# A two-layer graph kernel: one-hot stationary, gathered rows moving, node-major sums in groups of 8 tiles, a register load on TensorE with each tile

## The chip, the core and the metric

The kernel runs on one core of a Trainium2 chip. The core has five engines with a queue of instructions each: TensorE (PE; its weight loads are listed as PEld), VectorE (DVE), ScalarE (ACT), GpSimd (POOL) and SyncE (SP, which only issues transfers). They meet through semaphores. The metric is the device time of one execution in microseconds (us), the median of several runs.

## The reference, cut to what matters

There are 12500 nodes with 256 features and 200000 edges from `src` to `dst`, sorted by `dst`. Two layers follow each other; each ends in a residual and a layer norm:

```
# layer 0
t1  = x @ W1
msg = (t1[src] + (x[src] * x[dst]) @ W2) / (sqrt(deg[src]) * sqrt(deg[dst]))
agg = segment_sum(msg, dst)
x1  = layernorm(x + l2_normalise(leaky_relu(where(in_cnt > 0, t1 + agg, 0) + b0)))
# layer 1
out = segment_sum((x1 @ W.T + b1)[src], dst) / (in_deg + 1)
y   = layernorm(x1 + out)
```

Both layers reduce to one thing that is costly: for each edge a row of 256 float32 is fetched by `src`, and the rows of one `dst` are added. In layer 0 the fetched row is x divided by the root of its node's degree, in layer 1 it is x1. The matrix products come after the sum, once per node.

## The kernel before

**Tiles.** The edges are cut into tiles of 128, padded to 1568. A round is U = 32 tiles, and each layer has ROUNDS = 49 of them. One round belongs roughly to 256 nodes (two blocks of 128), since the edges are sorted.

**The gathers (POOL).** For each tile one indirect DMA (`gather_quarter`, L408) fetches 128 rows of 1 KB into one of the 32 places of `ring`. GpSimd reads the 128 row numbers from `idx`, a tile in SBUF. `idx` has 32 columns; ACT fills 8 of them at a time from `src_col` (`refill`, L523) as soon as TensorE has used the 8 tiles that stood in these places of the ring. The last round of a layer has FINAL = 27 tiles of gathers. The first 28 tiles of layer 0 are fetched unscaled from x, and with them their factors (`gather_r`, L416), before the scaled table is stored; the other 4 of round 0 come from the table.

**The sums (DVE, PE, DVE).** For a group of GT = 4 tiles DVE makes a one-hot tile of 64 columns each (`group_hot`, L715, both inputs in SBUF), TensorE multiplies (L1034): the gathered rows are the stationary operand, in two halves of 128 features, and the one-hot of 64 columns moves. The result is feature-major: 128 features by 64 nodes, for each half. DVE adds it to the accumulator `big` at a place that it loads into a register (`load_base`, L738; `add_group`, L743). Two buffers in PSUM take turns.

**The rest of layer 0.** In each round DVE also makes two batches of bf16 one-hots of dst's digits (`hot_batch`, L598, two instructions a batch), TensorE multiplies them (L940) and DVE adds the counts to `deg` (L829): this is the in-degree.

**The nodes.** One round later the sums of two blocks are finished: TensorE turns x (L997, L999), DVE mixes it with the sums (L753, L755), TensorE multiplies with the weights (`products`, L1013), DVE and ACT normalise (L768 to L823), SP stores. In layer 1, ACT copies the sums (L537) to be the stationary operand. Layer 1 starts when the last block of layer 0 is stored (POOL waits for SP, L327). TensorE multiplies all 32 tiles of the last round too; for the last 5 it only doesn't wait for a gather.

**What sets the order.** Each engine's program is written out by hand; nothing is planned by costs. Before the rounds (0 to 240 us) the edges are turned, degrees counted, x scaled and stored as a table.

Of the kernel before, what the change touches and what calls it, by code (L numbers as in the profile page):

```python
# [35 lines left out]
GT = 4  # L36
GR = U // GT
GROUPS = TILES // GT
WIN = 64
ACC_N = NPAD + WIN  # L40
# [8 lines left out]
HBATCHES = TILES // HB  # L49
# [6 lines left out]
LAST_K = 2  # L56
AHEAD = 3
HOTS = 4
QT = U // 4
# [4 lines left out]

RAW = 7 * GT
RAW_EARLY = [u for u in range(RAW) if 3 <= u < 13 or 20 <= u < 26]
RAW_LATE = [u for u in range(RAW) if u not in RAW_EARLY]
RAW_FIRST = 3
FIRST_GROUPS = 3
# [3 lines left out]
def gnn(nc, x, src, dst, w1, w2, b0, wl, b1, out):  # L73
# [3 lines left out]
    base_dram = nc.dram_tensor("group_bases", (BLOCKS * U,), I32, kind="Internal").ap()  # L77
    sums_dram = [nc.dram_tensor(f"sums{n}", (NPAD + P, D), F32, kind="Internal").ap() for n in range(2)]

    with ExitStack() as ctx:  # L80
# [3 lines left out]
        def sem(name):  # L84
# [3 lines left out]
        big = sb("big", [P, KF * ACC_N])  # L88
        acc = big[:, :].rearrange("p (k n) -> p k n", k=KF)
        x_all = big[:, 0:NW * D].rearrange("p (w f) -> p w f", w=NW)  # L90
        ring = sb("ring", [P, U, D])
# [7 lines left out]
        src_digits = ring_flat[:, 2 * BLOCKS * P:3 * BLOCKS * P].bitcast(BF16)  # L99
        lo = [src_digits[:, 0:TILES], sb("dst_lo", [P, TILES + HB], BF16)[:, :]]  # L100
        hi = [src_digits[:, TILES:2 * TILES], sb("dst_hi", [P, TILES + HB], BF16)[:, :]]
        count_to = sb("count_to", [P, P, PAIR], BF16)
        hot = sb("hot", [P, 2, HB // PAIR, P + HI, PAIR], BF16)
# [3 lines left out]
        steps = ring_flat[:, 4 * BLOCKS * P:].bitcast(BF16)[:, 0:3 * SB * (P + HI)].rearrange(  # L107
            "p (n t j) -> p n t j", n=3, t=SB)
        step_digits = nat[0][:, 0:2 * STEP_TILES].rearrange("p (d t) -> p d t", d=2)
        digit_t = hot[:, :, :, :, :].rearrange("p a b c d -> p (a b c d)")[:, 0:2 * TILES].bitcast(I32)  # L110
        win_iota = sb("win_iota", [P, WIN])
        dst_hot = sb("dst_hot", [P, HOTS, GT, WIN])
# [5 lines left out]
        zeros = sb("zeros", [P, D])  # L118
        dump_row = sb("dump_row", [P, 1])
        epsilon = sb("epsilon", [P, 1])  # L120
        bounds = sb("bounds", [P, 2, BLOCKS])
        gmin = sb("gmin", [BLOCKS, U])
        gmax = sb("gmax", [BLOCKS, U])
        floor_i = sb("floor_i", [BLOCKS, U], I32)
        floor_late = sb("floor_late", [BLOCKS, U // GR, GR - LAST_K - 1], I32)
        floor_f = sb("floor_f", [BLOCKS, U])
        gmin_i = sb("gmin_i", [BLOCKS, U], I32)
        bad = sb("bad", [BLOCKS, 4])
        flag = sb("flag", [1, 1], I32)
        base_row = sb("base_row", [1, BLOCKS * U], I32)  # L130
        base_row_f = dst_hot[0:1, 0:2, :, :].rearrange("p a b c -> p (a b c)")[:, 0:BLOCKS * U]
# [3 lines left out]
        r_diag = [sb(f"r_diag{n}", [P, P]) for n in range(2)]  # L135
        columns = r_diag[0]
        deg = sb("deg", [P, NW])
# [6 lines left out]
        a_t = [sb(f"a_t{n}", [P, KF, P]) for n in range(2)]  # L144
        out_t = [sb(f"out_t{n}", [P, D]) for n in range(2)]
        sums_t = sb("sums_t", [P, D])
        sum_a = a_t
        xa = [sb(f"xa{n}", [P, KF, P]) for n in range(2)]
# [11 lines left out]
        def group_sum(buf):  # L160
            return banks[:, 2 * buf:2 * buf + 2, 0:WIN]
# [3 lines left out]
        turned = [banks[:, 5 + s, :].rearrange("p (a k n) -> p a k n", a=2, k=KF) for s in range(2)]  # L165
        project = [banks[:, 7, 0:D], banks[:, 5, 0:D]]
# [38 lines left out]
        raw_turn = sem("raw_turn")  # L205

        r_edges_in = [sem(f"r_edges_in{n}") for n in range(2)]
# [18 lines left out]
        x_turned = sem("x_turned")  # L226
        sums_turned = sem("sums_turned")
        mixed = sem("mixed")
        hist_added = sem("hist_added")
# [878 lines left out]
```

## Time and profile before

| what | value |
|---|---|
| timed runs | median 4266.98 us of 3 (4265.9 to 4276.45) |
| profiled execution | 4292.12 us, span of its instructions 4290.4 us |
| busy PE | 3621.7 us (84%), PEld 3168.4 (74%) |
| busy POOL | 3140.3 us (73%) |
| busy DVE | 1600.2 us (37%) |
| busy ACT | 381.6 us (9%) |
| DMA | 489.92 MB, 114 GB/s over the span |
| mean granted TensorE clock | 0.595 of 2.4 GHz |

The profiled execution is slower than the median of the timed runs by 25.1 us; its durations are used against its own time. "Busy" counts an engine's instructions without their issue; a busy share is an average over stages. For POOL the span between two gathers is not counted as busy. The chain of waits says which work ended last, step by step, and that is what an edit has to shorten. The first 240 us are preparation, layer 0's rounds run from there to about 2271 us, layer 1's to the end.

### The profile page before, as it was taken

The numbers are of one execution on the slowest core, as the hardware profiler recorded it, in microseconds if no ns is written. First come the engines' busy times: TensorE is split into PE (matmuls) and PEld (weight loads), VectorE is DVE, ScalarE is ACT, GpSimd is POOL, SyncE is SP. The second block draws the span as 40 slices with busy tenths as digits, with TensorE's granted clock in tenths as the row PEclk, the third lists the DMA queues.
The fourth block names the chain that finished last, engine by engine and source line by source line (L and its number), as shares of the span: only waits on it lengthen the run. The fifth ranks groups of instructions, "written<-read, shape, count | busy, mean of one in ns | idle before, by whom it ended". The sixth has DMA issues, their size and how long they took to land.

```text
span 4290.4 us, 60042 instructions
## 1 busy us (share of the span) xinstructions
PE 3621.7 (84%) x17483; PEld 3168.4 (74%) x17483; DVE 1600.2 (37%) x4104; ACT 381.6 (9%) x1359; POOL 3140.3 (73%) x3175
## 2 busy tenths in 40 slices
PE   6578888888888888888887888888888888888888
PEld 5477777877777777777776777777777777767776
DVE  9954444444444444444442222222222222222222
ACT  8800000000000000000000000000000000000000
POOL 2277777777777777777776777777777777777776
PEclk8755656666566656666565555555555555555555
DMA  5243333333333333343433344343343433434433
GB/s 164 87 129 115 111 115 113 112 115 110 115 110 116 111 114 115 110 115 109 116 109 98 112 117 117 112 116 113 116 117 112 117 114 114 118 111 117 117 113 104
DMA packets 236973, 489.92 MB, mean 114 GB/s; under 512 B 57537, under 2 KB 136916, under 8 KB 236948
## 3 DMA queue, kind: packets, MB, share of 16 engines
q0 software_dynamic: 150944, 409.95, 33.6%
q1 hardware_dynamic: 86004, 79.66, 5.8%
q8 instruction: 13, 0.21, 0.0%
q14 instruction: 12, 0.10, 0.0%
HBM read 450.84 MB, written 38.54 MB: 114 GB/s over the span
## 4 chain that ended last, share of the span: by engine, by line
POOL 69%; issue 25%; DVE 3%; PE 2%; POOLq 1%; DMA 0%; DVEq 0%; SPq 0%; ACT 0%; ACTq 0%
POOL ring L408 68%; DVE hot L598 2%; PE banks L1034 1%; POOL r_edge L416 1%; POOLq L444 0%; POOL ring L412 0%; PE banks L940 0%; POOLq L405 0%; PE banks L1013 0%; POOLq L406 0%; DVEq L590 0%; DVEq L640 0%; DMA ring<-in_dst 0%; PE banks L999 0%; DMA ring<-scaled_x,idx 0%
## 5 line engine op out<-in xcount | busy, mean ns | idle before, releaser
L1034 PE MATMUL banks<-dst_hot,ring 128*128 128x64 f32 x12544 | 2949.5, 395 | 562.5 <-DMA ring<-x,idx 250.8
L1034 PEld LDWEIGHTS banks<-dst_hot,ring 128*128 128x128 f32 x12544 | 2576.2, 294 | 938.3 <-DMA ring<-x,idx 377.0
L408 POOL DMA_INDIRECT ring<-x,idx x1563 | 1525.4, 976 | 499.2 <-issue 476.2
L408 POOL DMA_INDIRECT ring<-scaled_x,idx x1535 | 1539.4, 1003 | 467.9 <-issue 467.3
L743 DVE TENSOR_TENSOR big<-banks,big 128x128 f32 x784 | 228.7, 292 | 1936.8 <-PE banks L1034 1934.7
L715 DVE TENSOR_TENSOR dst_hot<-win_iota,dst_rel 128x256 f32<-128x256 f32 x787 | 337.0, 428 | 311.1 <-issue 310.9
L523 ACT COPY idx<-src_col 128x8 int32 (+1 forms) x392 | 77.5, 198 | 2875.4 <-PE banks L1034 2875.3
L940 PE MATMUL banks<-hot 128*128 128x98 bf16 x2848 | 210.7, 241 | 47.9 <-DVE hot L598 47.1
L940 PEld LDWEIGHTS banks<-hot 128*128 128x128 bf16 x2848 | 194.1, 120 | 67.6 <-DVE hot L598 44.8
L1013 PE MATMUL banks<-wt_s,a_t 128*128 128x256 f32 x392 | 179.0, 637 | 1.3 <-ACT a_t L537 1.3
L598 DVE TENSOR_TENSOR hot<-ring,count_to 128x2048 bf16<-128x2048 bf16 (+1 forms) x160 | 162.0, 1094 | 0.2
L491 ACT ACTIVATE ring<-r_diag,ring 128x128 bf16<-128x128 f32 x576 | 161.3, 389 | 4.6 <-DVE ring L634 4.6
L412 POOL DMA_INDIRECT ring<-in_x,idx x28 | 38.7, 1381 | 155.0 <-DVE r L663 133.1
L598 DVE TENSOR_TENSOR hot<-dst_lo,count_to 128x2048 bf16<-128x2048 bf16 x99 | 121.9, 1231 | 72.4 <-issue 72.3
L1013 PEld LDWEIGHTS banks<-wt_s,a_t 128*128 128x128 f32 x392 | 125.6, 335 | 27.8 <-ACT a_t L537 1.5
L1013 PE MATMUL banks<-w_s,xa 128*128 128x256 f32 x392 | 121.2, 438 | 0.0
L1013 PE MATMUL banks<-w_s,a_t 128*128 128x256 f32 x392 | 106.8, 397 | 0.0
L999 PE MATMUL banks<-r_diag,x_t 128*128 128x128 f32 x392 | 102.8, 417 | 0.0
L598 DVE TENSOR_TENSOR hot<-dst_hi,count_to 128x1568 bf16<-128x1568 bf16 x99 | 95.9, 969 | 0.0
L999 PEld LDWEIGHTS banks<-r_diag,x_t 128*128 128x128 f32 x392 | 95.4, 333 | 0.0
L1013 PEld LDWEIGHTS banks<-w_s,a_t 128*128 128x128 f32 x392 | 82.1, 209 | 14.0
L1013 PEld LDWEIGHTS banks<-w_s,xa 128*128 128x128 f32 x392 | 80.9, 218 | 10.1
(118 smaller groups left out, 1043.4 us busy)
## 6 DMA issues: line engine op xcount, KB each, us to landing
ring<-x,idx POOLq DMA_INDIRECT x1563, 2.8
ring<-scaled_x,idx POOLq DMA_INDIRECT x1535, 2.8
x<-out_t SPq DMA_DIRECT2D x98, 128.0 KB
x_t<-x SPq DMA_DIRECT2D x98, 128.0 KB, 2.2
big<-in_x SPq DMA_DIRECT2D x1, 12416.0 KB
x_t<-in_x SPq DMA_DIRECT2D x97, 128.0 KB, 2.2
result<-out_t SPq DMA_DIRECT2D x97, 128.0 KB
scaled_x<-big SPq DMA_DIRECT2D x6, 1792.0 KB, 13.8
```

The source lines that it names most:

```text
L408: g.indirect_dma_start(ring[:, u, :], None, table[layer], bass.IndirectOffsetOnAxis(ap=idx[:, u:u + 1], axis=0)).then_inc(rows_in[u], 16)
L412: g.indirect_dma_start(ring[:, u, :], None, x, bass.IndirectOffsetOnAxis(ap=idx[:, u:u + 1], axis=0)).then_inc(rows_in[u], 16)
L416: g.indirect_dma_start(r_edge[:, u:u + 1], None, r_dram, bass.IndirectOffsetOnAxis(ap=idx[:, u:u + 1], axis=0)).then_inc(r_edges_in[n], 16)
L491: last = nc.scalar.activation(steps[:, third, t, first:first + size], columns[:, 0:size], ACT.Sign, bias=step_digits[:, digit, bass.ds(n * ...
L523: nc.scalar.copy(idx[:, q * QT:(q + 1) * QT], src_col[:, bass.ds(i * U + U + q * QT, QT)]).then_inc(idx_ready, 1)
L598: last = nc.vector.tensor_tensor(hots[half], vals.unsqueeze(2).to_broadcast(shape), count_to[:, 0:size, :].unsqueeze(1).to_broadcast(shape ...
L715: last = nc.vector.tensor_tensor(dst_hot[:, buf, :, :], win_iota[:, :].unsqueeze(1).to_broadcast([P, GT, WIN]), rel, ALU.is_equal)
L743: nc.vector.tensor_tensor(here, group_sum(k % 2), here, ALU.add).then_inc(groups_added, 1)
L940: last = nc.tensor.matmul(hist, lo_hot[half][:, t // PAIR, :, t % PAIR], hi_hot[half][:, t // PAIR, :, t % PAIR], start=first and t == 0, ...
L999: last = nc.tensor.matmul(turned[s][:, 1, k, :], x_t[s][:, k * P:(k + 1) * P], r_diag[s][:, :], start=True, stop=True)
L1013: last = nc.tensor.matmul(project[s], left, right, start=k == 0, stop=k == len(parts) - 1)
L1034: last = nc.tensor.matmul(group_sum(k % 2)[:, f, :], ring[:, u, f * P:(f + 1) * P], dst_hot[:, k % HOTS, j, :], start=j == 0, stop=j == GT ...
```

## The change

- The one-hot becomes the stationary operand (128 edges by 128 nodes), and the gathered row moves (257 columns: 256 features and a column of ones, set once in `ring`, whose places are now 264 wide). One float32 matmul a tile instead of two. The sums come out node-major, and column 256 counts the edges of a node, so the batches of bf16 one-hots, their matmuls and `deg` go in the rounds.
- A group is GT = 8 tiles, 4 groups a round. `group_hot` makes 8 one-hots of 128 columns in one instruction of 1024 elements; its first input is now a row in PSUM (`lane_row`), and what is compared is dst's low 7 bits. A group of 8 may span two blocks of 128 nodes: `add_group` adds it to both, with a mask for each, in two instructions of 257 elements. Four PSUM buffers take turns.
- x is no longer turned and mixed feature-major. DVE mixes in node-major form (`mix`), TensorE turns the mixed halves (`turn_halves`, after tile 20 of a round), ACT copies them from PSUM (`take_turned`), and TensorE multiplies (`products`, after tile 24).
- Round 0 of layer 0 is fetched unscaled as a whole (32 tiles, and 32 gathers of factors behind `r_stored`).
- The last round's matmuls stop with its 27th tile.
- After each tile, TensorE loads one register from memory (`pace`); the value isn't used.

```diff
-GT = 4
+GT = 8
-WIN = 64
+DW = D + 1
+PITCH = 264
-LAST_K = 2
+LAST_K = 1
+TURN_U = 20
+MIX_U = 24
+SUMS = 4
-RAW = 7 * GT
+RAW = U
...
         def group_sum(buf):
-            return banks[:, 2 * buf:2 * buf + 2, 0:WIN]
+            return banks[:, buf, 0:DW]
...
             g.wait_ge(step_digits_made, 1)
-            for u in RAW_EARLY:
-                gather_raw(u)
-            g.wait_ge(r_made, 1)
-            for u in RAW_LATE[:RAW_FIRST]:
+            for u in range(RAW):
                 gather_raw(u)
             g.wait_ge(r_stored, 16)
-            for u in RAW_LATE[:RAW_FIRST] + RAW_EARLY:
-                gather_r(u, 0)
-            for u in RAW_LATE[RAW_FIRST:]:
-                gather_raw(u)
-            for u in RAW_LATE[RAW_FIRST:]:
-                gather_r(u, 1)
+            for u in range(RAW):
+                gather_r(u)
...
             def refill(layer, i, q):
 
-                act.wait_ge(tiles_done, (layer * ROUNDS + i) * U + q * QT + QT + U)
+                act.wait_ge(groups_done, group_no(layer, i, q) + 1)
...
+            def take_turned(layer, m):
+                parts = 2 if layer == 0 else 1
+                for s in range(2):
+                    act.wait_ge(halves_turned, 2 * node_no(layer, m) + s + 1)
+                    if s == 0:
+                        act.wait_ge(projected, 2 * node_no(layer, m) + 2)
+                    act.sem_inc(act_turn, 1)
+                    nc.scalar.copy(a_t[s][:, 0:parts, :, :].rearrange("p h k n -> p (h k n)"),
+                                   turned[s][:, 0:parts * D]).then_inc(a_ready[s], 1)
...
             def group_hot(first_tile, buf, raw=False):
 
-                rel = dst_rel[:, bass.ds(first_tile, GT)].unsqueeze(2).to_broadcast([P, GT, WIN])
+                rel = dst_rel[:, bass.ds(first_tile, GT)].unsqueeze(2).to_broadcast([P, GT, P])
                 last = nc.vector.tensor_tensor(dst_hot[:, buf, :, :],
-                                               win_iota[:, :].unsqueeze(1).to_broadcast([P, GT, WIN]),
+                                               lane_row.unsqueeze(1).to_broadcast([P, GT, P]),
                                                rel, ALU.is_equal)
...
-            def add_group(layer, i, k, base):
-                v.wait_ge(tiles_done, group_no(layer, i, k) * GT + GT + U)
-                here = acc[:, :, bass.ds(base, WIN)]
-                nc.vector.tensor_tensor(here, group_sum(k % 2), here, ALU.add).then_inc(groups_added, 1)
+            def add_group(layer, i, k, block):
+
+                v.wait_ge(groups_done, group_no(layer, i, k) + 1)
+                for n in range(2):
+                    here = big[:, bass.ds((block + n) * DW, DW)]
+                    last = nc.vector.scalar_tensor_tensor(here, group_sum(k), here_mask[:, n, bass.ds(i * GR + k, 1)],
+                                                          here, ALU.mult, ALU.add)
+                last.then_inc(groups_added, 1)
+
+            def mix(m, sums):
+
+                two = bass.ds(2 * m, 2)
+                nc.vector.scalar_tensor_tensor(pair[0], sums[:, :, D], 0.0, r[:, two], ALU.is_gt, ALU.mult)
                 for s in range(2):
+                    v.wait_ge(x_in[s], 16 * (m + 1))
+                    nc.vector.scalar_tensor_tensor(halves[:, s, 0, :], x_t[s][:, :], root[:, bass.ds(2 * m + s, 1)],
+                                                   sums[:, s, 0:D], ALU.mult, ALU.add)
+                    nc.vector.tensor_tensor(halves[:, s, 1, :], x_t[s][:, :], sums[:, s, 0:D],
+                                            ALU.mult).then_inc(mixed, 1)
...
                     ordered()
-
-                    if layer == 0 and k in (0, 3):
-                        half = k // 3
-                        hot_batch(SRC_BATCHES + 2 * i + half + 1, 2 * i + half + 1, 1 - half, 1)
-                    if layer == 0 and k % 4 == 1:
-                        add_hist(SRC_BATCHES + 2 * i + k // 4)
...
+                    if finish and k >= LAST_K:
+                        done = acc[:, bass.ds(2 * i - 2, 2), :]
+                        if k == LAST_K and layer == 0:
+                            mix(i - 1, done)
+                        if k == LAST_K + 1:
+                            finish_sums(layer, i - 1, done)
+                            moments(layer, i - 1)
+                        if k == LAST_K + 2:
+                            norm(layer, i - 1)
...
+            def pace():
+
+                pe.value_load(block_row[0:1, 0:1], min_val=0, max_val=NW - 1)
...
                 for k in range(GR):
-                    if layer == 0 and k in (0, GR // 2):
-                        half = k // (GR // 2)
-                        dst_hist(SRC_BATCHES + 2 * i + half, half)
                     pe.wait_ge(dst_hot_made, group_no(layer, i, k) + 1)
                     pe.wait_ge(groups_added, group_no(layer, i, k) + 1)
-                    for j in range(GT):
-                        u = k * GT + j
-                        if u < end:
-                            rounds_before = layer * (ROUNDS if u < FINAL else ROUNDS - 1) + i
-                            pe.wait_ge(rows_in[u], 16 * (rounds_before + 1))
-                        for f in range(KF):
-                            last = nc.tensor.matmul(group_sum(k % 2)[:, f, :], ring[:, u, f * P:(f + 1) * P],
-                                                    dst_hot[:, k % HOTS, j, :], start=j == 0, stop=j == GT - 1)
-                        last.then_inc(tiles_done, 1)
...
+                    tiles = range(k * GT, min((k + 1) * GT, end))
+                    for u in tiles:
+                        rounds_before = layer * (ROUNDS if u < FINAL else ROUNDS - 1) + i
+                        pe.wait_ge(rows_in[u], 16 * (rounds_before + 1))
+                        last = nc.tensor.matmul(group_sum(k), dst_hot[:, k % HOTS, u - k * GT, :], ring[:, u, 0:DW],
+                                                start=u == tiles[0], stop=u == tiles[-1])
+                        if u == tiles[-1]:
+                            last.then_inc(groups_done, 1)
+                        pace()
+                        if finish and u == TURN_U - 1:
+                            turn_halves(layer, i - 1)
+                        if finish and u == MIX_U - 1:
+                            products(layer, i - 1)
```

How the instructions stand on VectorE in the loop over layer 0's rounds, from the top of a round, first before (one group of 4 tiles with a batch of bf16 one-hots; ISA and REGISTER_ALU rows are waits, signals and register work; `hot` is that batch, `base_row` the register load):

```order
L715 TENSOR_TENSOR dst_hot<-win_iota,dst_rel 128x256
L741 REGISTER_ALU
L743 ISA
L743 TENSOR_TENSOR big<-banks,big 128x2x64
L738 ISA
L738 TENSOR_LOAD base_row
L738 ISA x2
L594 ISA
L598 ISA
L598 TENSOR_TENSOR hot<-dst_lo,count_to 128x8x256
L598 REGISTER_ALU
L598 TENSOR_TENSOR hot<-dst_hi,count_to 128x8x196
```

and now, one group of 8 tiles (`hot_space` holds the one-hots, `banks` is PSUM):

```order
L710 TENSOR_TENSOR hot_space<-banks,dst_rel 128x1024
L733 REGISTER_ALU
L736 ISA
L736 SCALAR_TENSOR_TENSOR big<-banks,here_mask,big 128x257
L736 ISA
L736 REGISTER_ALU
L736 SCALAR_TENSOR_TENSOR big<-banks,here_mask,big 128x257
L729 ISA
L729 TENSOR_LOAD block_row
L729 ISA x2
```

The batch is gone, the one-hot instruction is longer and its first input is in PSUM, and the add is two instructions. On TensorE in the same loop, before, two groups with what stands between them (turning x):

```order
L1034 MATMUL banks<-dst_hot,ring 128x64 x8
L994 ISA
L995 REGISTER_ALU
L997 MATMUL banks<-ident,x_t 128x128 x2
L999 MATMUL banks<-r_diag,x_t 128x128 x2
L997 MATMUL banks<-ident,x_t 128x128 x2
L999 MATMUL banks<-r_diag,x_t 128x128 x2
```

and now, around the turn in the middle of the third group (the waits are on the rows in the ring and on the mixed halves):

```order
L1004 MATMUL banks<-ring,hot_space 128x257
L993 TENSOR_LOAD block_row
L993 ISA x2
L971 ISA
L977 MATMUL banks<-ident,halves 128x128 x4
L971 REGISTER_ALU
L977 MATMUL banks<-ident,halves 128x128 x4
```

Each tile is one matmul row instead of two, and each is followed by a register load and two more instructions of the sequencer.

## Rows read from the trace of the kernel before

**Rows 1.** The page, chain that ended last, shares of the span.

```profile
POOL 69%; issue 25%; DVE 3%; PE 2%; POOLq 1%; DMA 0%; DVEq 0%; SPq 0%; ACT 0%; ACTq 0%
```

**Rows 2.** Waits of POOL: us in total, times, longest.

```profile
POOL ring L408 <- issue: 943.6, 3095, 0.3
POOL ring L412 <- DVE r L663: 133.1, 1, 133.1
POOL ring L408 <- SPq L327: 22.9, 1, 22.9
```

**Rows 3.** Line L408, all gathers of the rounds: duration min/median/max, first and last start.

```profile
L408 POOL DMA_INDIRECT ring<-x,idx x1563: 945/949/1217, 2270.6 to 4271.3; - x196
L408 POOL DMA_INDIRECT ring<-scaled_x,idx x1535: 945/949/1972, 240.7 to 2246.8; - x192
```

**Rows 4.** The page, costliest groups: busy us, mean ns, idle before.

```profile
L408 POOL DMA_INDIRECT ring<-x,idx x1563 | 1525.4, 976 | 499.2 <-issue 476.2
L408 POOL DMA_INDIRECT ring<-scaled_x,idx x1535 | 1539.4, 1003 | 467.9 <-issue 467.3
```

**Rows 5.** Timeline of layer 0, 302 to 307 us, POOL and DVE: start, us.

```profile
302.83 0.43 DVE L715 TENSOR_TENSOR dst_hot<-win_iota,dst_rel 128x256 f32<-128x256 f32 x1 [1.42 <-issue]
302.97 1.11 POOL L408 DMA_INDIRECT ring<-scaled_x,idx  x1 [0.30 <-issue]
...
304.09 1.23 DVE L598 TENSOR_TENSOR hot<-dst_lo,count_to 128x2048 bf16<-128x2048 bf16 x1 [0.62 <-issue]
304.39 1.75 POOL L408 DMA_INDIRECT ring<-scaled_x,idx  x1 [0.31 <-issue]
...
306.44 0.94 POOL L408 DMA_INDIRECT ring<-scaled_x,idx  x1 [0.30 <-issue]
306.49 0.29 DVE L743 TENSOR_TENSOR big<-banks,big 128x128 f32 x1
```

**Rows 6.** Timeline of layer 0, 655 to 658 us, POOL and DVE.

```profile
656.45 0.88 DVE L768 SCALAR_TENSOR_TENSOR e<-banks,scal,b_s 128x256 f32<-128x256 f32 x2
656.48 0.95 POOL L408 DMA_INDIRECT ring<-scaled_x,idx  x1 [0.30 <-issue]
```

**Rows 7.** Timeline, a round of layer 0: the slow gathers of 1028 to 1040 us.

```profile
1031.80 1.14 POOL L408 DMA_INDIRECT ring<-scaled_x,idx  x1 [0.30 <-issue]
...
1037.01 1.01 POOL L408 DMA_INDIRECT ring<-scaled_x,idx  x1 [0.30 <-issue]
```

**Rows 8.** The page, DVE's one-hots of the groups.

```profile
L715 DVE TENSOR_TENSOR dst_hot<-win_iota,dst_rel 128x256 f32<-128x256 f32 x787 | 337.0, 428 | 311.1 <-issue 310.9
```

**Rows 9.** Timelines of PE: four tiles of layer 0; products of layer 1.

```profile
1004.03 3.64 PE L1034 MATMUL banks<-dst_hot,ring 128*128 128x64 f32 x16
...
2989.85 3.73 PE L1013 MATMUL banks<-wt_s,a_t 128*128 128x256 f32 x8
```

**Rows 10.** Register loads by line: duration ns min/median/max, first and last start.

```profile
L738 DVEq FUSED_REGOPS  x1456: 57/190/194, 235.1 to 4276.9; - x182
L738 DVEq TENSOR_LOAD <-base_row x784: 299/305/329, 234.7 to 4276.6; - x196
...
L1047 PEldq TENSOR_LOAD <-flag x1: 1094/1094/1094, 209.3 to 209.3; - x1
```

**Rows 11.** Timeline, start of the rounds.

```profile
231.44 0.36 DVE L715 TENSOR_TENSOR dst_hot<-win_iota,dst_rel 128x256 f32<-128x256 f32 x1
...
232.36 7.09 PE L1034 MATMUL banks<-dst_hot,ring 128*128 128x64 f32 x32 [12.19 <-DVE dst_hot L723]
...
246.71 0.95 POOL L408 DMA_INDIRECT ring<-scaled_x,idx  x1 [0.30 <-issue]
```

**Rows 12.** Timeline, from layer 0 to layer 1.

```profile
2249.99 5.38 PE L1034 MATMUL banks<-dst_hot,ring 128*128 128x64 f32 x24 [0.57 <-DMA ring<-scaled_x,idx]
...
2261.43 0.48 DVE L768 SCALAR_TENSOR_TENSOR e<-banks,scal,b_s 128x256 f32<-128x256 f32 x1 [1.24 <-PE banks L1013]
...
2270.63 0.95 POOL L408 DMA_INDIRECT ring<-x,idx  x1 [22.93 <-SPq L327]
```

More of the change, by code:

```diff
@@ L48 @@
 PAIR = 2
-HBATCHES = TILES // HB
 SB = 4
@@ L441, in _ @@
                         g.wait_ge(table1_whole, 1)
[L442 to L443 removed]
+                    if layer == 1:
+                        for q in range(4):
+                            gather_quarter(layer, 0, q)
                     with g.Fori(1, ROUNDS - 1) as i:
@@ L872, in _ @@
                     if layer == 0:
-                        for s in range(2):
-                            mix(ROUNDS - 1, s, acc[:, :, (NW - 2 + s) * P:(NW - 1 + s) * P])
-                    for step in (finish_sums, moments, norm):
-                        step(layer, ROUNDS - 1)
+                        mix(ROUNDS - 1, acc[:, NW - 2:NW, :])
+                    finish_sums(layer, ROUNDS - 1, acc[:, NW - 2:NW, :])
+                    moments(layer, ROUNDS - 1)
+                    norm(layer, ROUNDS - 1)
             with v.Else():
@@ L1003, in products @@
-            def products(layer, m, s, taken):
-                if layer == 0:
-                    pe.wait_ge(mixed, 2 * m + 2 if s == 1 else 2 * m + 1)
-                    parts = [(xa[s][:, k, :], w2_s[:, k, :]) for k in range(KF)]
-                    parts += [(sum_a[s][:, k, :], w1_s[:, k, :]) for k in range(KF)]
-                else:
-                    pe.wait_ge(a_ready[s], taken + 1)
-                    parts = [(a_t[s][:, k, :], wt_s[:, k, :]) for k in range(KF)]
-                for k, (left, right) in enumerate(parts):
-                    last = nc.tensor.matmul(project[s], left, right, start=k == 0, stop=k == len(parts) - 1)
-                last.then_inc(projected, 1)
@@ L1016, in dst_hist, with turn_halves @@
-            def dst_hist(n, half):
-                pe.wait_ge(hist_added, n - SRC_BATCHES + 1)
-                hist_batch(n, half, True, True)
+            def turn_halves(layer, m):
+                for s in range(2):
+                    if layer == 0:
+                        pe.wait_ge(mixed, 2 * m + s + 1)
+                    elif s == 0:
+                        pe.wait_ge(sums_taken, m + 1)
+                    for h in range(2 if layer == 0 else 1):
+                        for k in range(KF):
+                            place = (h * KF + k) * P
+                            last = nc.tensor.transpose(turned[s][:, place:place + P], halves[:, s, h, k * P:(k + 1) * P],
+                                                       ident[:, :])
+                    last.then_inc(halves_turned, 1)
@@ new lines, in products @@
+            def products(layer, m):
+                weights = (w1_s, w2_s) if layer == 0 else (wt_s,)
+                for s in range(2):
+                    pe.wait_ge(a_ready[s], node_no(layer, m) + 1)
+                    parts = [(a_t[s][:, h, k, :], w[:, k, :]) for h, w in enumerate(weights) for k in range(KF)]
+                    for n, (left, right) in enumerate(parts):
+                        last = nc.tensor.matmul(project[s], left, right, start=n == 0, stop=n == len(parts) - 1)
+                    last.then_inc(projected, 1)
@@ L1037, in round_ @@
-                    if finish and layer == 0 and k == LAST_K:
-                        for s in range(2):
-                            turn_x(i - 1, s)
-                    if finish and k == LAST_K + 1:
-                        for s in range(2):
-                            products(layer, i - 1, s, i - 1)
+                    tiles = range(k * GT, min((k + 1) * GT, end))
[11 more added lines that the diff above has]
+                            products(layer, i - 1)
```

359 lines of the change are left out of this document (148 added, 211 removed).

## Prediction

> **What bounds the kernel now.** I read the chain of waits first [rows 1]: POOL holds 69% of it and its issue another 25%. The list of POOL's waits [rows 2] says that it is never fed late in the rounds: behind the preparation (133.1 us, once) the only long wait is 22.9 us between the layers; the other 943.6 us are 3095 gaps of about 0.305 us between one gather and the next. So the time is a row of gathers, and the view by line [rows 3] gives the clean step: median 949 ns plus 305 ns, 1.254 us. 1535 gathers lie between 240.7 and 2246.8 us, 1563 between 2270.6 and 4271.3.
>
> The means [rows 4] are above the median: 1003 ns in layer 0 and 976 in layer 1. That is (1003 − 949) × 1535 = 82.9 us and (976 − 949) × 1563 = 42.2 us of stretched gathers. The clean step plus this stretch gives back both stretches of time: 1534 × 1.254 + 82.9 = 2006.6 us against 2246.8 − 240.7 = 2006.1, and 1562 × 1.254 + 42.2 = 2000.9 against 2000.7. Nothing else is in them.
>
> What stretches a gather is seen in the timeline [rows 5]. The gather that starts at 302.97, while DVE's L715 (both inputs in SBUF) runs to 303.26, takes 1.11 us; the one at 304.39, with L598 running to 305.32, takes 1.75. The excess over 0.949 fits a wait until about where the DVE instruction ends. The gather at 306.44 beside L743, whose first input is in PSUM, takes 0.94, and the one at 656.48 beside the long L768 (0.88 us, input in PSUM) takes 0.95 [rows 6]. So a DVE instruction holds a gather up only when it reads two tensors in SBUF, as far as these rows go.
>
> TensorE is busy 84% of the time but not bounding: four tiles of 16 passes take 3.64 us [rows 9], 0.91 a tile, below 1.254.
>
> **The change part by part.**
>
> *Number of gathers and first start.* Layer 0's round 0 is now all unscaled. Its gathers of rows fall in POOL's 133.1 us of waiting [rows 2]; the 32 gathers of factors end, by my estimate of 1.25 us each, just ahead of the tables' being ready. Round 1's first gather needs group 0's matmuls. Before, the matmuls of 8 tiles started at 232.36, took 7.09, and round 1's fetching starts at 246.71, behind 4 gathers for round 0 [rows 11]. Now: memsets done as before at about 231.44, a one-hot of 1024 elements, 4 times that of 256. L715's 256 elements take 428 ns in the mean, 337.0 / 787 [rows 8], 0.36 here; 4 times 0.36 less fixed cost is 1.26 us, and two of them give 234.0. Then 8 tiles of matmuls: before each tile took 4 passes of 64 columns, now 2 of 257, and products of 256 columns take 3.73 / 8 = 0.47 us a pass with their end [rows 9], so about the same 7.1 for 16 passes. With ACT's refill and the issue that is 242. Gain 4.7 us.
>
> *Layer 0's row of gathers.* From round 1 there are 47 × 32 + 27 = 1531 gathers, 1530 steps × 1.254 = 1918.6 us. The batches L598 and the one-hots L715 with two SBUF inputs are gone; the new one-hot and both adds have one tensor in PSUM. What still reads two in SBUF is some 10 small instructions a round (in `mix` and the norm). Their price I take from a round of layer 0 where two gathers away from L598 and L715 took 1.14 and 1.01 us [rows 7]: 0.19 + 0.06 = 0.25 us over the 6 such instructions of a round, 0.04 each. 10 × 49 × 0.04 = 20 us. Bounds: 0, and 42.2 us over layer 1's 490 two-input instructions of before, 0.086 each, so 42 us. I take 20, since the small ones are the nearest kin.
>
> *Layer 1's.* 1562 × 1.254 = 1958.7; 2 such instructions a round, 98 × 0.04 = 4 us, bounds 0 and 8.4.
>
> *The register load on TensorE.* The trace before has no such load with each tile. DVE's L738 does the same (a value of a row in SBUF) 784 times at 299 to 329 ns with a 190 ns instruction behind it; TensorE's own, L1047, is there once, 1094 ns, at 209.3 us in the traffic of the preparation [rows 10]. A tile then costs TensorE's queue 0.31 + 0.19 us and the issue of a matmul and a wait, 0.15 to 0.4 by estimate: 0.65 to 0.9, beside two passes of 257 columns, at most 2 × 0.47 = 0.93 by L1013 [rows 9], and I take 0.86, since the 3.73 us hold the end of the last pass too. If load and passes lay behind one another it would be 0.31 + 0.86 = 1.17 and more; if beside, 0.9. Nothing in the load needs the array, so I take 0.9. A round of layer 0 holds 32t plus 8.5 us for the turn (8 transposes, 1.7 by estimate) and the products (16 passes, 6.8 at 0.43); POOL needs 32 × 1.254 + 0.4 = 40.5. At t = 0.9 that is 37.3: cover of 3 us. The cover ends at t = 1.0 in layer 0; in layer 1 (4.6 us of extra) at 1.11. Stalls within a round are buffered by the ring: 24 tiles × 1.254 = 30 us of rows ahead, less 2.8 for landing.
>
> The Trainium skill, page "DMA: Bandwidth & Descriptors", section "Latency and other measured facts", gives a register load from memory a floor of about 600 ns. The trace disagrees: 784 loads at 299 to 329 ns on VectorE [rows 10], and the measurement decides. With 0.6 + 0.19 + 0.35 one would have t = 1.14 and, by the sum of the first rival below, about 4,430 us.
>
> *DVE and ACT off the path.* The adds and one-hots are hidden: in a round of 40 us DVE has 4 × (1.26 + 2 × 0.4) us (0.29 for L743's 128 elements [rows 5], so about 0.4 for 257) and some 10 us for the nodes. ACT is called per 8 tiles as before.
>
> *Between the layers.* Before: the last tiles' matmuls start at 2249.99 for 5.38 (24 passes, with 5 empty tiles that go now), the norm at 2261.43, the first gather of layer 1 at 2270.63 [rows 12]: 20.6 from 2249.99. Now the last pair's path has its sums first on DVE and then turned: products and finish of the pair before 2.5 + 5.5, one-hot 1.3, adds 0.9, factors 1.2, mix 1.2, transposes 1.0, ACT's copy 0.6, products 5.2 (16 passes, at most 7.5 by L1013's 3.73 for 8 and half of that at the higher clock), and 9.2 from the norm (2270.63 − 2261.43): 28.6. So +8 us (+5 to +12): 23.8 becomes about 32.
>
> *End.* 4290.4 − 4271.3 = 19.1 us, unchanged by the same counting (−1 to +7).
>
> *Sum.* 242 + 1918.6 + 20 = 2180.6; + 32 = 2212.6; + 1958.7 + 4 = 4175.3; + 19.1 = 4194.4, 96 us under the span of 4290.4. With 1.7 us around the span the profiled time is 4196.1. The medians stand to that as 4266.98 / 4292.12 = 0.9941: 4171.5 us, I say 4171. With no stretch, 4147; with the upper prices and the gap and tail at their worst, 4202. Own range 4140 to 4202.
>
> **The rivals.**
>
> 1. *TensorE becomes the bound through the register load* (slower side). Place: between two tiles in its queue. It decides above t = 1.0, in layer 0 alone at first, and from t = 1.06 the kernel is no longer faster: 49 × (32 × 1.06 + 8.5 − 40.5) = 95 us, the whole gain. Above 1.11 each 0.1 us of t costs 64 × 49 × 0.1 = 314 us. With load and passes in series, t = 1.17: 4171 + 49 × (64 × 1.17 + 8.5 + 4.6 − 40.5 − 40.2) = 4,528. With L1047's 1.094 behind some 0.5 us, t = 1.6: 4171 + 49 × 34.8 = 5,876. For it: the only load on this engine was 1.09 us, and nothing shows that a load and passes run side by side. Against: 784 loads at 0.3, and that one lay in heavy traffic. Chance 0.12. A mild form, t from 1.0 to 1.06, ends at 4175 to 4265: 0.08.
> 2. *The new long one-hot holds POOL up after all.* Its `dst_rel` is in SBUF and it runs 1.26 us, 392 times; if the PSUM operand doesn't free the path, each hit costs half its length by the rows of L598 [rows 5], 0.31 to 0.63 us: 123 to 250 us, 4,290 to 4,417. For: L743's case is a short instruction. Against: L768's at 0.88 us [rows 6]. Chance 0.07.
> 3. *The stretch isn't DVE's but there anyway* (traffic): then only start and gaps change, and the time is 4171 + 101 = about 4,272, no change. Against: the excess ends with the DVE instruction. It is in the remaining 0.03.
>
> **How the numbers follow.** The forecast has 0.70, so 4171. Within 0.3%, about 13 us either way, a measurement of this kernel can't tell from no change; faster means under 4254. The forecast's 0.70, three quarters of the mild form and a little of the rest give 0.77; same 0.04; slower 0.12 + 0.07 = 0.19. The range of 8 in 10 is 4135 to 4260: the forecast's own and the mild form, 0.78, and the edges.
>
> **What would show it.** Right: L408's median at 0.95 and means below 0.97 in both layers, POOL's only waits the one before round 1 and one of about 32 us between the layers, round 1's first gather near 242, and TensorE's loads near 0.3 us with its steps of tiles following POOL's 1.25. Wrong: POOL waiting for ACT's `idx` behind TensorE's groups throughout, which is rival 1; gathers of over 1.3 us beside the one-hot of 1024 elements, rival 2; a mean of 1003 still there with neither, rival 3. Steps of tiles of TensorE with load and passes in series at over 1.0 us would make it wrong even with short loads.

## The result: 2.2% faster, and the profile after

The kernel after the change takes 4174.5 us (median of 4 runs, 4171.9 to 4178.56), the kernel before beside it 4269.35 (4265.9 to 4276.45). The ratio is 0.9777, 95% interval 0.976 to 0.9794. The forecast was 4171, faster. The profiled execution took 4172.7 us, its span 4170.9.

The page of the kernel after, its chain of waits by engine, answers to [rows 1]:

```profile
POOL 68%; issue 25%; DVE 4%; PE 1%; DVEq 1%; POOLq 1%; DMA 0%; SPq 0%; ACT 0%; ACTq 0%
```

It is the same row of gathers. The next lines are the waits of POOL after (total us, times, longest), which answer to [rows 2]:

```profile
POOL ring L405 <- issue: 941.5, 3091, 0.3
POOL r_edge L413 <- DMA r_table<-e: 102.7, 1, 102.7
POOL ring L405 <- SPq L327: 29.8, 1, 29.8
POOL ring L409 <- DVE halves L629: 14.3, 1, 14.3
POOL ring L405 <- ACT idx L514: 10.7, 2, 10.4
```

After the start, POOL waits only between the layers. Then the gathers themselves by line (min/median/max, first and last start), against [rows 3]:

```profile
L405 POOL DMA_INDIRECT ring<-x,idx x1563: 942/946/1211, 2190.5 to 4151.9; - x196
L405 POOL DMA_INDIRECT ring<-scaled_x,idx x1531: 942/946/1227, 238.8 to 2159.7; - x192
```

and their sums and means from the page, against [rows 4], with the new one-hot:

```profile
L405 POOL DMA_INDIRECT ring<-x,idx x1563 | 1486.5, 951 | 505.7 <-issue 475.9
L405 POOL DMA_INDIRECT ring<-scaled_x,idx x1531 | 1455.9, 951 | 476.4 <-issue 465.6
...
L710 DVE TENSOR_TENSOR hot_space<-banks,dst_rel 128x1024 f32<-128x1024 f32 x395 | 483.7, 1224 | 198.1 <-issue 197.6
```

The means fell from 1003 and 976 ns to 951: of 82.9 + 42.2 us of stretch, (951 − 946) × 3094 = 15.5 us are left. The longest gather is 1.23 us where it had been 1.97.

The forecast's sum, term by term (us; "after" from the first and last starts above and the span):

| part | forecast | after |
|---|---|---|
| first gather of round 1 | 242 | 238.8 |
| layer 0's row, first to last start | 1938.6 | 1920.9 |
| last gather of layer 0 to first of layer 1 | 32 | 30.8 |
| layer 1's row | 1962.7 | 1961.4 |
| last gather to the end | 19.1 | 19.0 |
| span | 4194.4 | 4170.9 |

The span was forecast 23.5 us too long. The forecast then took 24.6 us off again by the factor 0.9941, since the profiled execution of before was that much slower than its median. The profiled execution of after is not slower (4172.7 against 4174.5). So the nearness of 4171 to 4174.5 is two misses that cancel: the mechanism was right, and each of the two sizes was about 24 us, 0.6%, off. That nearness is luck.

### The profile page after: what moved, and what is told of

It reads as the page before. It is cut to its first block, busy times and chain, and to the rows that moved or that the text cites. A ratio compares the mean times of both kernels' runs of the same rounds, so it can differ in the third digit from the quotient of the medians.

```text
span 4170.9 us, 49033 instructions
## 1 busy us (share of the span) xinstructions
PE 3387.3 (81%) x9623; PEld 1749.8 (42%) x9623; DVE 1603.1 (38%) x3315; ACT 460.4 (11%) x1457; POOL 3033.6 (73%) x3179
## 4 chain that ended last, share of the span: by engine, by line
POOL 68%; issue 25%; DVE 4%; PE 1%; DVEq 1%; POOLq 1%; DMA 0%; SPq 0%; ACT 0%; ACTq 0%
POOL ring L405 68%; DVE hot_space L600 2%; DVEq L592 0%; PE banks L1004 0%; DVE big L663 0%; PE banks L988 0%; POOLq L435 0%; POOLq L402 0%; PE banks L916 0%; DVE big L724 0%; POOLq L403 0%; DVEq L635 0%; DMA ring<-in_dst 0%; SPq L270 0%; DMA ring<-x,idx 0%
## 5 line engine op out<-in xcount | busy, mean ns | idle before, releaser
L1004 PE MATMUL banks<-ring,hot_space 128*128 128x257 f32 x6252 | 2901.9, 575 | 671.6 <-DMA ring<-x,idx 326.5
L1004 PEld LDWEIGHTS banks<-ring,hot_space 128*128 128x128 f32 x6252 | 1315.7, 256 | 2192.9 <-DMA ring<-x,idx 1045.3
L405 POOL DMA_INDIRECT ring<-x,idx x1563 | 1486.5, 951 | 505.7 <-issue 475.9
L736 DVE SCALAR_TENSOR_TENSOR big<-banks,here_mask,big 128x257 f32 x784 | 343.7, 480 | 2086.7 <-PE banks L1004 2086.6
L710 DVE TENSOR_TENSOR hot_space<-banks,dst_rel 128x1024 f32<-128x1024 f32 x395 | 483.7, 1224 | 198.1 <-issue 197.6
L482 ACT ACTIVATE dst_rel<-columns,halves 128x128 bf16<-128x128 f32 x576 | 161.3, 374 | 4.5 <-DVE halves L629 4.5
L977 PE MATMUL banks<-ident,halves 128*128 128x128 f32 x588 | 131.2, 388 | 13.2 <-DVE halves L748 8.7
L977 PEld LDWEIGHTS banks<-ident,halves 128*128 128x128 f32 x588 | 112.8, 207 | 46.6 <-issue 23.0
L916 PE MATMUL banks<-hot_space 128*128 128x98 bf16 x1280 | 91.1, 236 | 40.0 <-DVE hot_space L600 39.2
L536 ACT COPY a_t<-banks 128x512 f32<-128x512 f32 (+1 forms) x196 | 90.4, 479 | 282.6 <-PE banks L977 282.2
L600 DVE TENSOR_TENSOR hot_space<-src_lo,count_to 128x2048 bf16<-128x2048 bf16 x80 | 97.6, 1221 | 0.2
L760 DVE SCALAR_TENSOR_TENSOR e<-banks,scal,b_s 128x256 f32<-128x256 f32 x98 | 42.9, 479 | 134.2 <-PE banks L988 134.2
```

The costliest lines, as they stand in the source:

```text
L405: g.indirect_dma_start(ring[:, u, 0:D], None, table[layer], bass.IndirectOffsetOnAxis(ap=idx[:, u:u + 1], axis=0)).then_inc(rows_in[u], 16)
L482: last = nc.scalar.activation(steps[:, third, t, first:first + size], columns[:, 0:size], ACT.Sign, bias=step_digits[:, digit, bass.ds(n * ...
L536: nc.scalar.copy(a_t[s][:, 0:parts, :, :].rearrange("p h k n -> p (h k n)"), turned[s][:, 0:parts * D]).then_inc(a_ready[s], 1)
L600: last = nc.vector.tensor_tensor(hots[half], vals.unsqueeze(2).to_broadcast(shape), count_to[:, 0:size, :].unsqueeze(1).to_broadcast(shape ...
L710: last = nc.vector.tensor_tensor(dst_hot[:, buf, :, :], lane_row.unsqueeze(1).to_broadcast([P, GT, P]), rel, ALU.is_equal)
L736: last = nc.vector.scalar_tensor_tensor(here, group_sum(k), here_mask[:, n, bass.ds(i * GR + k, 1)], here, ALU.mult, ALU.add)
```

## The experiments

Twelve kernels were run, in three lots on three chips, each lot with the kernel before beside it: 4269.0 us in the first, 4272.0 in the second, 5097.7 in the third. Ratios are to that one, with 95% intervals.

**1. Where the inputs of VectorE's instructions lie.** The kernel after, with the one operand moved back to SBUF:

```diff
-        lane_row = banks[:, 7, 0:P]
+        lane_row = sb("lane_sb", [P, P])[:, :]
```

> The kernel after with the first input of the one-hot (L710) in SBUF in place of PSUM, so that it reads two tensors in SBUF; nothing else. My theory: a gather that begins beside it waits until it ends; 392 of 1.22 us, a gather begins every 1.25, so nearly each is hit once and waits some 0.6 us: + 230 us, about 4,400, half in each layer, with gathers of 1.0 to 2.1 us beside L710. Rival (what stretched gathers before was the length, the bf16 type or chance traffic and not where the inputs lie): 4174.

Measured: 4285.6 us, ratio 1.0047 (1.0031 to 1.0062), that is + 111 us against the 4174.5 of the first result, and all of the change's gain is gone. The page of this kernel, its gathers and the one-hot; below it two pieces of its timeline (start, duration in us):

```profile
L405 POOL DMA_INDIRECT ring<-x,idx x1563 | 1520.2, 973 | 504.8 <-issue 475.8
L405 POOL DMA_INDIRECT ring<-scaled_x,idx x1531 | 1536.0, 1003 | 472.0 <-issue 465.6
...
L710 DVE TENSOR_TENSOR hot_space<-lane_sb,dst_rel 128x1024 f32<-128x1024 f32 x395 | 484.0, 1225 | 197.6 <-issue 197.1
```

```profile
1018.51 1.23 DVE L710 TENSOR_TENSOR hot_space<-lane_sb,dst_rel 128x1024 f32<-128x1024 f32 x1 [0.19 <-issue]
1018.71 1.85 POOL L405 DMA_INDIRECT ring<-scaled_x,idx  x1 [0.31 <-issue]
...
1039.29 1.22 DVE L710 TENSOR_TENSOR hot_space<-lane_sb,dst_rel 128x1024 f32<-128x1024 f32 x1 [1.23 <-issue]
1039.84 1.50 POOL L405 DMA_INDIRECT ring<-scaled_x,idx  x1 [0.30 <-issue]
```

The one-hot takes as long as with the operand in PSUM (1225 and 1224 ns), but the gather that starts 0.20 us behind it takes 1.85 us, the one 0.55 behind it 1.50: both end 0.82 and 0.83 us after the one-hot does (1019.74 and 1040.51). The direction is the theory's, the price half of what it said, and it isn't split evenly between the layers. I had spread the hits evenly over the instruction (0.6 us each), while the one-hot starts at a few places against the gathers. Counted in the trace, 194 gathers began beside it in layer 0, with 0.54 us of it left in the mean, and took 0.41 us more than the median of 0.946; in layer 1 it was 194 too, with 0.28 us left, and they took 0.17 more. That is 79 + 33 = 113 us, the whole of what the operand cost.

Then the same from the other side, on the kernel before: its batches left out (TensorE and the add go on with old one-hots, so these kernels leave out layer 0's in-degrees, which the outputs need), its one-hot with a first input in PSUM, and both.

```diff
-                        hot_batch(SRC_BATCHES + 2 * i + half + 1, 2 * i + half + 1, 1 - half, 1)
+                        v.wait_ge(hot_used, SRC_BATCHES + 2 * i + half + 2)
+                        v.sem_inc(hot_made, 1)
```

> The kernel before without the two bf16 one-hot instructions of each batch in the rounds (98 x 2 of layer 0; TensorE's matmuls and the add of counts stay and work on old one-hots, so the in-degrees are not computed). My theory: the gathers that waited for them get 61.6 us back in layer 0 and nothing in layer 1: about 4208. Rival (gathers are long because of traffic): 4269.

```diff
-        project = [banks[:, 7, 0:D], banks[:, 5, 0:D]]
+        project = [banks[:, 6, 0:D], banks[:, 5, 0:D]]
+        win_row = banks[:, 7, 0:WIN]
...
-                                               win_iota[:, :].unsqueeze(1).to_broadcast([P, GT, WIN]),
+                                               win_row.unsqueeze(1).to_broadcast([P, GT, WIN]),
...
+            nc.vector.tensor_copy(win_row, win_iota[:, :])
...
-                    pe.wait_ge(mixed, 2 * m + 2 if s == 1 else 2 * m + 1)
+                    pe.wait_ge(mixed, 2 * m + 2)
```

> The kernel before with the first input of its one-hot (L715 of before) in PSUM; the product of the first block goes to another bank for it and waits for both mixed blocks. My theory: the waits beside L715 go, 9 us in layer 0 and 39 in layer 1: about 4221. Rival: 4269.

> Both edits of the kernel before at once (in-degrees not computed). My theory: the two gains add, 62 + 48 = 110 us: about 4160, that is slightly below the kernel after, with the old number of matmuls, no register loads and the old gap between the layers. If the gain of the change lay in its matmuls or node-major sums, it would stay at 4210 or above.

Measured: without the batches 4217.6 us, 0.9869 (0.9854 to 0.9884), − 54; with the operand in PSUM 4216.3, 0.9864 (0.9849 to 0.9879), − 56; both 4169.5, 0.9757 (0.9743 to 0.977), − 102.5. The pages' gather rows, first without the batches, then with the operand in PSUM, then both:

```profile
L408 POOL DMA_INDIRECT ring<-x,idx x1563 | 1523.6, 975 | 500.3 <-issue 475.7
L408 POOL DMA_INDIRECT ring<-scaled_x,idx x1535 | 1472.8, 959 | 467.8 <-issue 466.9
```

```profile
L409 POOL DMA_INDIRECT ring<-scaled_x,idx x1535 | 1510.3, 984 | 467.7 <-issue 467.4
L409 POOL DMA_INDIRECT ring<-x,idx x1563 | 1482.8, 949 | 502.2 <-issue 476.0
```

```profile
L409 POOL DMA_INDIRECT ring<-x,idx x1563 | 1482.1, 948 | 501.5 <-issue 475.9
L409 POOL DMA_INDIRECT ring<-scaled_x,idx x1535 | 1460.8, 952 | 467.6 <-issue 467.3
```

Without the batches only layer 0's mean falls (1003 to 959); with the operand in PSUM layer 1's falls most (976 to 949), though layer 0's falls too (1003 to 984), more than the 9 us that I had given it. The single gains, 54 and 56 us, were expected as 62 and 48, and together they gave a little less than their sum of 110. Counted gather by gather in the trace of the kernel before, those that began beside a batch (L598) in layer 0 lost 65 us, those beside the one-hot (L715) 9 us in layer 0 and 40 in layer 1: 115 of the 125 us of stretch. Both together bring the kernel before, with its old matmuls, its old sums and no register loads, to 4169.5 us: within the intervals as fast as the kernel after. This shows where the 2.2% came from: no batches, and the one-hot's row in PSUM. The new shape of the product gave time only in that it needs no batches; the row in PSUM could be had without it.

**2. The register load on TensorE.** None, two and three in place of one behind each tile; with two:

```diff
                         pace()
+                        pace()
```

> The kernel after without the register load behind each tile. My theory: POOL alone sets the time, so 4174 us, within 5 us either way, and means of L405 of 951 ns as before. Rival: the load gives something back (it keeps TensorE's clock up, 0.72 against 0.60 before, or spaces its reads of SBUF away from the gathers); then without it the granted clock falls to about 0.60 and either the gaps between the layers and at the end grow by some 2 to 5 us each (4180), or gathers get longer again (4200 and more).

> Two register loads behind each tile. A load with its two followers takes 302 + 146 + 18 = 466 ns of TensorE's queue, a tile step in a burst is 0.66 us in the kernel after, so 1.13 here. My theory (loads and passes side by side, the ring as buffer): layer 0's round takes 32 x 1.13 + 6.5 = 42.7 us against POOL's 40.1, layer 1's about 40.2, so + 2.6 x 49 = 127 us: about 4300, POOL waiting for idx in layer 0 and hardly in layer 1. Rival 1: TensorE has slack up to 1.25 a tile because turn and products overlap the loads: 4174. Rival 2: loads and passes behind one another, 0.86 + 0.93: about 5,600.

> Three register loads behind each tile: t = 0.66 + 2 x 0.466 = 1.59. My theory: (32 x 1.59 + 6.5 - 40.1) + (32 x 1.59 + 4 - 40.1) = 32.1 us over both layers' rounds, x 49 = 1573: about 5,750, every further 0.466 us costing 64 x 49 x 0.466 = 1461 us. Rival (serial): about 7,000.

Measured: none 4168.6 us, 0.9768 (0.9754 to 0.9781); two 4556.9, 1.0678 (1.0662 to 1.0695); three 6594.2, 1.5453 (1.5425 to 1.5481). None and one are not told apart: the intervals of the ratios overlap, though the slowest of five executions without the load (4170.7) is below the fastest of four with it (4171.9), in another lot. The unchanged kernel was run once more to settle these 6 us (part 3) and met a slow chip, so they stay open. The profiled spans are 4169.0 and 4170.9 us, the mean granted clocks 0.713 and 0.719. So the load doesn't raise the clock either; that it is above the 0.595 of before comes with the other edits.

Two and three cost far more than I had said (4300 and 5750). The waits of POOL with two, and with three:

```profile
POOL ring L405 <- issue: 887.2, 2803, 4.6
POOL ring L405 <- ACT idx L514: 404.3, 290, 14.1
```

```profile
POOL ring L405 <- ACT idx L514: 2422.2, 377, 18.7
...
POOL ring L405 <- issue: 867.6, 2716, 9.1
```

and the loads with two, in 5 us of layer 0's rounds (ns min/median/max, first and last start in us):

```profile
L993 PEldq TENSOR_LOAD <-block_row x8: 298/301/302, 994.3 to 999.0; - x8
L993 PEldq FUSED_REGOPS  x8: 146/146/146, 994.6 to 999.4; - x8
L993 PEldq SEQ_ASSERT  x7: 18/18/18, 994.8 to 998.9; - x7
```

Eight loads start from 994.3 to 999.0, 0.67 us apart, though the three instructions of one last only 0.465 us together: the spaces between them belong to the price. With two loads a tile takes 2 × 0.67 = 1.34 us, and the gathers' starts say the same: layer 0's 1530 steps take 2092.8 us, 1.37 each, layer 1's 1562 take 2113.7, 1.35; with three it is 2.02 and 1.99. My step had been 1.13, from durations alone. A round of 32 such tiles would be 42.9 us, and 32 steps measured 43.8 and 43.3: the turn and the products, which I had added with 6.5 us, lie nearly all beside the queue's time. That these steps are the queue's and not the passes' is seen at the start of the rounds, where the rows lie ready. Without a load 80 passes, 40 tiles, take 20.21 us there, 0.51 us a tile, while with one load a tile takes 0.68:

```profile
231.42 20.21 PE L1004 MATMUL banks<-ring,hot_space 128*128 128x257 f32 x80 [20.68 <-DVE hot_space L717]
```

So TensorE has two limits a tile, about 0.5 us for its passes and 0.67 us of its queue for each load, and it binds when the larger passes POOL's 1.25. With one load nothing is near that.

**3. One idle VectorE instruction more,** behind each of the 392 one-hots, to compare kinds of instruction; the operands lie in a part of SBUF that the rounds don't use. One of these lines is added (`s_a` and `s_b` are `src_lo` and `src_hi` read as float32):

```diff
+                    nc.vector.tensor_tensor(s_a, s_a, s_b, ALU.mult)
...
+                    nc.vector.tensor_scalar(s_a, s_b, 1.0, None, ALU.mult)
...
+                    nc.vector.tensor_tensor(src_lo[:, :], src_lo[:, :], src_hi[:, :], ALU.mult)
```

> The kernel after once more, unchanged, beside the three below on one chip: ratio to the kernel before 0.977 to 0.979, 4170 to 4178 us. If it comes nearer 0.9768, the 6 us between the first result and the kernel without the register load were noise.

> The kernel after with one idle VectorE instruction more behind each of the 392 one-hots: a float32 product of two SBUF tensors of 784 elements, 0.9 us; its result is not used. My theory (two tensors in SBUF hold a gather up): by the 111 us that 392 instructions of 1.22 us cost in the kernel with the SBUF operand, and by hits spread evenly, 60 to 125 us: about 4,260. Rival (it was something else about that operand): 4174.

> The same with a tensor_scalar of one SBUF tensor of 784 float32 elements. My theory: no gather waits, 4174. Rival: it takes the second port in a doubled mode, as the Trainium skill, page 'SBUF - State Buffer', section 'Who interferes with whom', says that tensor_scalar can; then it is some 0.5 us long and costs 392 x 0.4 (share that is hit) x 0.25 = 40 us: about 4,215.

> The same with a bf16 product of two SBUF tensors of 1568 elements, about 0.97 us by the instruction of that size in the preparation. My theory: the batches of the kernel before cost 54 us for 196 instructions, 0.28 each; 392 x 0.28 = 110 us: about 4,285. Rival (bf16 instructions hold only half of the gathers they meet, as the tally of before may say: 0.34 us lost where 0.85 was left): about half as much as the float32 product.

Measured, on a chip where both kernels were slow: before 5097.7 us; after, unchanged, 5044.5, 0.9889 (0.9866 to 0.9911); with the float32 product 5163.9, 1.0104 (1.0067 to 1.0141); with tensor_scalar 5074.1, 0.9952 (0.9934 to 0.9971); with the bf16 product 5169.7, 1.012 (1.0076 to 1.0163). Against the unchanged kernel that is + 119, + 30 and + 125 us. The executions of one kernel spread widely there, by 34 us for the unchanged one, 87 for the float32 product, 11 for tensor_scalar and 65 for the bf16 product. The page of the float32 product is that of its longest, 5198.1 us. The gathers and the added instruction on the pages or by line: the unchanged kernel, then with the float32 product, with tensor_scalar, and with the bf16 product:

```profile
L405 POOL DMA_INDIRECT ring<-scaled_x,idx x1531 | 1456.8, 952 | 961.7 <-ACT idx L514 510.9
L405 POOL DMA_INDIRECT ring<-x,idx x1563 | 1481.2, 948 | 889.2 <-issue 481.6
```

```profile
L406 POOL DMA_INDIRECT ring<-x,idx x1563 | 1533.4, 981 | 861.1 <-issue 449.8 <-ACT idx L515 366.1 <-SPq L328 45.2
L406 POOL DMA_INDIRECT ring<-scaled_x,idx x1531 | 1508.8, 986 | 1009.2 <-ACT idx L515 555.2 <-issue 454.1
L829 DVE TENSOR_TENSOR src_lo<-src_lo,src_hi 128x784 f32<-128x784 f32 x392 | 379.8, 969 | 0.0
```

```profile
L406 POOL DMA_INDIRECT ring<-x,idx x1563 | 1504.4, 963 | 876.4 <-issue 490.3 <-ACT idx L515 345.6 <-SPq L328 40.5
L406 POOL DMA_INDIRECT ring<-scaled_x,idx x1531 | 1473.8, 963 | 963.9 <-ACT idx L515 499.1 <-issue 464.8
L829 DVE TENSOR_SCALAR src_lo<-src_hi 128x784 f32<-128x784 f32 x392 | 228.4, 583 | 0.0
```

```profile
L406 POOL DMA_INDIRECT ring<-x,idx x1563 | 1533.0, 981 | 846.7 <-issue 456.9 <-ACT idx L515 345.6 <-SPq L328 44.2
L406 POOL DMA_INDIRECT ring<-scaled_x,idx x1531 | 1505.3, 983 | 1012.1 <-ACT idx L515 556.2 <-issue 456.0
L829 DVE TENSOR_TENSOR src_lo<-src_lo,src_hi 128x1568 bf16<-128x1568 bf16 x392 | 379.6, 968 | 0.0
```

The gathers' means say which instruction holds them up: 948 and 952 unchanged, 981 and 986 with two float32 tensors in SBUF, 981 and 983 with two of bf16, 963 with one tensor. So at equal length (969 and 968 ns) the type made no difference, and "only two tensors in SBUF" was too narrow: with the tensor_scalar of one tensor the gathers take (963 − 948) × 1563 + (963 − 952) × 1531 = 40 us more. Not all of that is waiting: in this profile, and in that of the float32 product, the median gather takes 949 ns in place of 946, which is 9 us over 3094 gathers. The 31 us that are left agree with the + 30 of the times. For the two products the same count gives 94 and 99 us, less than + 119 and + 125; on this chip the rest isn't accounted for. The tensor_scalar runs 583 ns where the product needs 969 for as many elements. The Trainium skill, page "SBUF — State Buffer", section "Who interferes with whom", says that tensor_scalar can enter a doubled mode that takes the ports GpSimd uses; the shorter run and the longer gathers agree with that, and my theory did not.

The times themselves are a weaker witness. On this chip POOL waits 510.9 us for `idx` in layer 0 of the unchanged kernel, behind TensorE, which it did for 10.7 us on the chip of the first result, though the gathers take the same 946 ns (median). TensorE itself stood for 1646.8 us before its sums (L1004), up to 10.0 at a time, and the profile names nothing that it waited for; in the first result it waited 597.0 us there, for rows to land. The bound is partly another one there; what slows that chip wasn't settled, and half of the change's gain is gone on it. The expectation of 0.977 to 0.979 for the unchanged kernel was missed.

**4. A version that beats both:** no register load, b1 in PSUM so that L781 (layer 1's `e`) reads one tensor in SBUF, and turn and products earlier.

```diff
-TURN_U = 20
-MIX_U = 24
+TURN_U = 18
+MIX_U = 20
...
+        b1_row = banks[:, 7, P:P + D]
...
-                        nc.vector.scalar_tensor_tensor(e[s][:, :], b1_s[:, :], scal[:, 4 + s:5 + s], x_t[s][:, :],
+                        nc.vector.scalar_tensor_tensor(e[s][:, :], b1_row, scal[:, 4 + s:5 + s], x_t[s][:, :],
...
-                        pace()
```

> The kernel after without the register loads, with b1 in PSUM (L781 then reads one tensor in SBUF), the turn after tile 18 and the products after tile 20. My theory: L781's 7.2 us of held gathers in layer 1 go; DVE ends the pair before the last some 2.6 us earlier, at each layer's end: 4174 - 7 - 5 = 4162. Rival: the earlier products make TensorE wait for the mix without gain: 4167 or, if that holds POOL up, above 4174.

Measured: 4162.2 us (4160.1 to 4162.4), 0.9739 (0.9725 to 0.9752), whose interval lies below that of the kernel after. Three edits were made at once, so the time alone doesn't say which gave what. In the kernel after, the timeline has L781 beside a gather in layer 1; below it are the gather rows on the best kernel's page:

```profile
3028.52 0.88 DVE L781 SCALAR_TENSOR_TENSOR e<-b_s,scal,x_t 128x256 f32<-128x256 f32 x2
3029.14 1.09 POOL L405 DMA_INDIRECT ring<-x,idx  x1 [0.30 <-issue]
```

```profile
L406 POOL DMA_INDIRECT ring<-x,idx x1563 | 1478.3, 946 | 504.9 <-issue 475.9
L406 POOL DMA_INDIRECT ring<-scaled_x,idx x1531 | 1456.2, 951 | 474.8 <-issue 463.9
```

Layer 1's mean falls from 951 to 946, 1486.5 − 1478.3 = 8.2 us, in the layer whose operand was moved. Layer 0's stays. The kernel with only the register load taken out still has 952 in layer 1, so the 8 us belong to the operand (or to the earlier products, which weren't run alone). Of the 5 us that I expected of earlier products little came: the wait between the layers is 29.0 us against 29.8.

## Why the prediction was right, point by point

- *The bound is the row of gathers, and a gather is stretched when VectorE reads two tensors in SBUF.* Right, and shown three ways: put back with one operand (+ 111 us), taken out of the kernel before with two edits (− 102.5), and instructions added alone. Too narrow by the tensor_scalar, whose kind was not among the rows that the prediction looked at.
- *The new 1.26 us one-hot holds nothing up* (against rival 2). Right: it takes 1224 ns, and 192 gathers that began beside it in layer 0 lost nothing in the mean. Rival 2's price of 123 to 250 us compares with the 111 that the SBUF operand measured.
- *20 + 4 us of small stretches.* Mis-sized: 5 ns × 1531 = 7.7 and 5 ns × 1563 = 7.8 us. Two gathers of one round [rows 7] were too few to price layer 0 from, and layer 1's 98 instructions L781 cost 7.3 us in the trace, 0.07 each, not 0.04.
- *A clean step of 1.254 us, and the ratio of median to profiled time on top.* The step measured 0.946 + 0.305 = 1.251. Of the 23.5 us by which the span was off, 3 ns × 3092 steps are 9, layer 0's smaller stretch 12, the start 3 and the gap 1, less 4 for layer 1's stretch; the rest is rounding. The 949 ns were most likely that one execution's: ten of the twelve kernels above show 946, two 949. The step that failed is the factor 0.9941, which takes it that a profiled execution is slower than the median as a rule. That of before was, by 25.1 us, that of after was not. Of the 25 the 949 ns are 9. More may lie in the batches: layer 0's row is 66.8 us shorter in the profile without them (2006.1 to 1939.3), while the medians differ by 54.4; but that is no second profile of the same kernel, and the cause stays open. The upper end of the own range was added up wrongly too: with the upper prices, the gap and the end all at their worst it is about 4209, not 4202, which leaves out the 7 us of the end.
- *Register load 0.31 us, beside the passes, t = 0.9.* Right in the load and in its lying beside the passes; the step of a tile was put too high. The median of 3126 on TensorE is 302 ns, and the first tiles, with rows in store, took 15.34 us for 45 passes, 0.68 a tile and not 0.9:

```profile
L993 PEldq TENSOR_LOAD <-block_row x3126: 296/302/758, 231.0 to 4155.0; - x196
```

```profile
230.98 15.34 PE L1004 MATMUL banks<-ring,hot_space 128*128 128x257 f32 x45 [20.70 <-DVE hot_space L717]
```

  The formula 32t + 8.5 was wrong for a round that the queue bounds, since turn and products don't add to it; by the kernels with two and three loads the cover reaches to about t = 1.25, further than I gave it. The floor of about 600 ns that the Trainium skill gives (page "DMA: Bandwidth & Descriptors", section "Latency and other measured facts") isn't the duration of a load here, 302 ns; the 0.67 us that a load takes of the queue, with its two followers and the spaces, is near it. Rival 1 is what the kernel with two loads does.
- *Between the layers + 8 us, the end unchanged.* 23.8 became 30.8, + 7; 19.1 became 19.0.

## What to carry to other kernels

Where GpSimd's gathers are the bound, look at each gather above the median and at what VectorE runs when it starts: a long instruction with two operands in SBUF cost time on the other engine here (a gather ended 0.82 us after it), a tensor_scalar of one did too, and one broadcast row moved to a spare PSUM bank saved 56 us of 4272 with little else changed. An addition to an engine's queue is priced by the distance between its starts, not by the durations of its parts, and set against that engine's own slack: the first register load cost at most some 6 us, the second cost 382 us. Before a forecast is scaled by a profile against a median, ask what in that one execution was slow.

## What the runs showed that was not expected

- A register load holds TensorE's queue for 0.67 us, of which 0.30 is the load.
- A tensor_scalar of one tensor raised the gathers' mean from 948 to 963 ns in layer 1, 3 ns of it in the median.
- One chip of three ran the kernel before in 5097.7 us instead of about 4270; there the same change gave 1.1%, not 2.2%.
